# Attention probabilities turned by VectorE block transposes and a DRAM exchange in place of TensorE transposes

## The reference

```
q = (x @ Wq) in 12 heads; k = (x @ Wk), v = (x @ Wv) in 3 heads, repeated 4 times
q, k = apply_rope(q), apply_rope(k)
attn = softmax(q @ k.T * SCALE)      # over the 128 keys (within the 256-key block)
out  = (attn @ v) @ Wo
h = h + attention(layernorm(h))
h = h + gelu(layernorm(h) @ in_weight.T + in_bias) @ out_weight
```

## Time and profile before

| what | value |
|---|---|
| median of 3 runs | 1157.02 us (1156.36 to 1157.75) |
| the profiled execution's own time | 1157.89 us |
| its span, first to last instruction | 1156.1 us |
| mean granted TensorE clock in it | 0.987 of full |
| busy: PE, PE weight load | 1096.8 us, 952.5 us |
| busy: DVE, ACT, POOL | 733.8 us, 758.2 us, 484.8 us |
| DMA | 26.79 MB moved, 23 GB/s over the span |

### The profile page before, as it was taken

The page is one execution under the profiler, slowest core; times in us unless marked ns, Lnnn a source line. Parts: engine busy times, 40 slices in busy tenths (PEclk is TensorE's granted clock), DMA queues, the critical chain, the costliest instruction groups (busy, mean ns, idle before and its releaser), DMA issues.

```text
span 1156.1 us, 24938 instructions
## 1 busy us (share of the span) xinstructions
PE 1096.8 (95%) x8000; PEld 952.5 (82%) x8000; DVE 733.8 (63%) x1999; ACT 758.2 (66%) x2532; POOL 484.8 (42%) x711
## 2 busy tenths in 40 slices
PE   3789999999999999999999999999999999999996
PEld 2578888888888888888888888888888888888875
DVE  3566666666676676676676666666666667667652
ACT  2456676766676766677766677676667676667763
POOL 0343534443444453443454353444344445344341
PEclk8889999999999999999999999999999999999999
DMA  5000101110010110010110010101000011001000
GB/s 158 19 19 9 26 18 25 25 25 7 25 25 18 25 25 16 16 25 18 25 25 25 7 25 18 25 25 25 7 25 22 22 25 25 9 23 25 0 8 14
DMA packets 47775, 26.79 MB, mean 23 GB/s; under 512 B 20752, under 2 KB 47248, under 8 KB 47760
## 3 DMA queue, kind: packets, MB, share of 16 engines
q1 hardware_dynamic: 45472, 23.46, 8.3%
q10 hardware_dynamic: 2288, 3.15, 0.8%
HBM read 20.30 MB, written 6.29 MB: 23 GB/s over the span
## 4 chain that ended last, share of the span: by engine, by line
PE 74%; DVE 8%; ACT 7%; issue 7%; POOL 3%; SPq 0%; DMA 0%; POOLq 0%; DVEq 0%
PE ring L780 11%; PE bank L698 11%; PE bank L640 11%; PE ring L653 8%; PE ring L677 8%; PE ring L609 7%; PE ring L630 5%; PE ring L663 3%; PE bank L721 2%; ACT t_e L300 2%; PE bank L751 2%; ACT t_q L281 2%; POOL rs L349 2%; DVE hn L442 2%; ACT HH L305 1%
## 5 line engine op out<-in xcount | busy, mean ns | idle before, releaser
L262 ACT ACTIVATE E<-ring,m_neg 128x128 f32<-128x128 f32 x768 | 270.5, 393 | 162.3 <-DVE m_neg L475 162.3
L374 POOL TENSOR_TENSOR E<-E,e_rcp 128x512 f32<-128x512 f32 x192 | 194.5, 1038 | 130.8 <-DVE e_rcp L488 130.7
L475 DVE TENSOR_REDUCE m_neg<-ring 128x4 f32<-128x512 f32 x192 | 120.5, 683 | 106.9 <-PE ring L653 106.9
L262 ACT ACTIVATION_READ_ACCUMULATOR E<-ring,m_neg 128x1 f32 x768 | 178.9, 233 | 0.0
L780 PE MATMUL ring<-wo_sb,OT 128*128 128x192 f32 x768 | 138.6, 330 | 0.3 <-ACT OT L274 0.3
L640 PE MATMUL bank<-wout_sb,G 128*128 128x192 f32 x768 | 138.3, 330 | 0.0
L358 POOL TENSOR_TENSOR q_tok<-rot_c,rot_s 128x384 f32<-128x384 f32 x128 | 125.5, 1000 | 7.8 <-DVE rot_s L464 7.8
L780 PEld LDWEIGHTS ring<-wo_sb,OT 128*128 128x128 f32 x768 | 124.7, 190 | 4.5 <-ACT OT L274 0.7
L640 PEld LDWEIGHTS bank<-wout_sb,G 128*128 128x128 f32 x768 | 123.2, 190 | 3.8
L347 POOL TENSOR_SCALAR ve<-mv 128x1 f32<-128x1 f32 x64 | 13.9, 217 | 242.2 <-DVE mv L438 242.2
L394 POOL TENSOR_SCALAR ve<-mv 128x2 f32<-128x2 f32 x32 | 7.3, 227 | 252.0 <-DVE mv L571 252.0
(11 more groups left out here) (110 smaller groups left out, 2567.2 us busy)
## 6 DMA issues: line engine op xcount, KB each, us to landing
x_sb<-in_x_dram SPq DMA_DIRECT2D x64, 192.0 KB, 2.5
out_dram<-out_sb SPq DMA_DIRECT2D x64, 96.0 KB, 2.3
x_sb<-in_x_dram SPq DMA_DIRECT2D x64, 64.0 KB, 2.4
w_raw<-in_w_att_dram ACTq DMA_DIRECT2D x2, 576.0 KB, 5.0
win_raw<-in_w_in_dram ACTq DMA_DIRECT2D x2, 384.0 KB, 6.1
wo_sb<-in_wo_dram ACTq DMA_DIRECT2D x1, 576.0 KB, 7.0
wout_sb<-in_w_out_dram ACTq DMA_DIRECT2D x1, 576.0 KB, 8.3
bqk_row<-in_bq_row_dram SPq DMA_DIRECT2D x1, 64.0 KB, 2.2
```

Source lines behind the costliest of these rows:

```text
L262: last = nc.scalar.activation(E[:, a, s * P:(s + 1) * P], RING[a][:, s * P:(s + 1) * P], ACT.Exp, bias=m_neg[:, a, s:s + 1], accum_out=e_s ...
L374: nc.gpsimd.tensor_tensor(e, e, r, ALU.mult).then_inc(prob_out, 1)
L475: nc.vector.tensor_reduce(m_neg[:, a, REP * g:REP * (g + 1)], RING[a][:, 512 * g:512 * (g + 1)].rearrange("p (h k) -> p h k", k=P), AX_X, ...
```

## The change

The turn of the probabilities leaves PE. Each group of 4 heads is transposed in 32x32 blocks by one DVE instruction from `E` to a new tile `EB`, ordered so that the column block comes first. SP writes `EB` to a DRAM scratch (`spill`), in two pieces for each sequence: heads 0 to 7 (128 partitions of 4 KB, 512 KB) and heads 8 to 11 (256 KB). SP reads each piece back to `ET` in four DMAs, one for each group of 32 partitions (128 KB or 64 KB each), which puts the blocks in their transposed places. Both the spills are issued before the first of the eight reads, and each read waits for its spill's semaphore. The 12 PE transposes of each sequence and the six copies of a step go. `probs_v` waits for the reads (`filled`), and reads `ET` through a view; `heads_out` undoes the order of columns.

The order of every engine is rewritten around it. On PE the steps that stood beside the turn move: `ffn_second(1)` goes to the following step behind `qkv(0)`, `scores(1)` comes before `tok_h` and `ffn_second(0)`, and `probs_v(0)` comes after them. There is one step more at the end (`NP + 1`), which holds only the last feed-forward result. On DVE the three maxima of the second sequence come before `h_next`. Banks `B6` and `B7` swap roles in part. ACT takes the four token-mixer bias steps before the first exponentials, and the scores of the mixer wait for them.

```diff
+        spill = nc.dram_tensor("spill", (2, P, NH * P), F32, kind="Internal").ap()
+            def blocks_moved(a, q):
+                for k, (s0, heads) in enumerate(PIECES):
+                    c = slice(s0 * P, (s0 + heads) * P)
+                    sp.wait_ge(blocks_out, 6 * q + 3 * a + 2 + k)
+                    need(sp, filled[k], 64 * (2 * (q - 1) + a + 1))
+                    sp.dma_start(spill[a, :, c], EB[:, a, c]).then_inc(spilled[k], 16)
+                for k, (s0, heads) in enumerate(PIECES):
+                    c = slice(s0 * P, (s0 + heads) * P)
+                    need(sp, pv_mm, 4 * (q - 1) + 2 * a + k + 1)
+                    sp.wait_ge(spilled[k], 16 * (2 * q + a + 1))
+                    for j in range(NB):
+                        sp.dma_start(ET[j * B32:(j + 1) * B32, a, c].rearrange("r (i e) -> r i e", i=NB),
+                                     spill[a, :, c].rearrange("(i r) (j e) -> j r i e", i=NB, j=NB)[j]
+                                     ).then_inc(filled[k], 16)
...
+                def blocks_turned(a, g, q):
+                    s0, heads = PIECES[g // 2]
+                    h0 = REP * g - s0
+                    dve.wait_ge(prob_out, 6 * q + 3 * a + g + 1)
+                    need(dve, spilled[g // 2], 16 * (2 * (q - 1) + a + 1))
+                    nc.vector.transpose(
+                        EB[:, a, s0 * P:(s0 + heads) * P].rearrange("p (j h c) -> p h j c", j=NB, h=heads)[:, h0:h0 + REP],
+                        E[:, a, 512 * g:512 * (g + 1)].rearrange("p (h j r) -> p h j r", h=REP, j=NB)
+                    ).then_inc(blocks_out, 1)
...
-                def probs_turned(a, g, q):
-                    pe.wait_ge(prob_out, 6 * q + 3 * a + g + 1)
-                    for s in range(REP * g, REP * (g + 1)):
-                        last = nc.tensor.transpose(RING[a][:, s * P:(s + 1) * P], E[:, a, s * P:(s + 1) * P], ident[:])
-                    last.then_inc(ET_mm, 1)
...
                 if ffn:
                     hn_turned()
-                if att:
-                    for g in range(NKV):
-                        probs_turned(0, g, p)
-                if ffn:
-                    ffn_first()
+                    ffn_first((0, 1))
...
                 if att:
-                    for g in range(NKV):
-                        probs_turned(0, g, p)
+                    key_max(1)
                 if tok:
                     dve.wait_ge(h_mm, n + 1)
```

More of the change, by code:

```diff
@@ L220, in store, with step @@
                                  out_sb[(1 - k) * D2:(2 - k) * D2]).then_inc(stored, 16)
+            def step(p, att, ffn, fin, more):
+                if ffn:
+                    blocks_moved(1, p - 1)
+                if fin:
+                    store(p - 2)
+                if more:
+                    load_ahead(p + 2)
+                if att:
+                    blocks_moved(0, p)
             load(0)
@@ L225, in _ @@
                 sp.dma_start(dst[:], src).then_inc(s_const, 16)
[L226 to L229, removed]
+            step(-1, False, False, False, True)
+            step(0, True, False, False, True)
+            step(1, True, True, False, True)
             with sp.Fori(2, NP - 2) as p:
[L231 to L234, removed]
+                step(p, True, True, True, True)
+            step(NP - 2, True, True, True, False)
+            step(NP - 1, True, True, True, False)
+            step(NP, False, True, True, False)
+            step(NP + 1, False, False, True, False)
             sp.wait_ge(stored, 32 * NP)
@@ L297, in step @@
                     tok_vq(0, B6)
+                    tok_vq(1, B7)
+                if att:
+                    score_exp(0, 0)
+                if ffn:
+                    heads_out(1, p - 1)
+                if att:
+                    score_exp(0, 1)
+                    score_exp(0, 2)
+                if tok:
                     act.wait_ge(s_max, n + 1)
@@ L322, in step @@
                     score_exp(1, 0)
+                    score_exp(1, 1)
+                    heads_out(0, p)
                 if tok:
@@ L572, in step @@
                 if att:
-                    dve.wait_ge(h_kept, p + 1)
-                    need(dve, h2_copied, p)
-                    residual(0, 2 * p + 1)
+                    sums_inverted(1, 0, p)
                 if tok:
@@ L610, in group, with step @@
                 return last
-            def step(p, att, tok, ffn):
+            def step(p, att, tok, ffn, fin):
                 n = p + 1
@@ L793, in step @@
                     qkv(0)
+                if fin:
+                    ffn_second(1, p - 2)
                 if tok:
@@ L796, in step @@
                     tok_qk()
-                if ffn:
-                    for g in range(NKV):
-                        probs_turned(1, g, p - 1)
                 if att:
                     qk_turned(0)
-                if ffn:
-                    probs_v(1, p - 1)
+                if tok:
+                    tok_vq()
                 if att:
@@ L813, in step @@
                     hn_turned()
+                    ffn_first((0, 1))
                 if att:
-                    for g in range(NKV):
-                        probs_turned(0, g, p)
+                    qk_turned(1)
                 if ffn:
-                    ffn_first()
+                    ffn_first((2,))
+                if tok:
+                    tok_probs_turned()
+                if att:
+                    scores(1)
+                if tok:
+                    tok_h()
+                if ffn:
+                    ffn_second(0, p - 1)
                 if att:
@@ L821, in step @@
                 if tok:
-                    tok_probs_turned()
-                if att:
-                    qk_turned(1)
-                if tok:
-                    tok_h()
+                    x_turned()
                 if att:
                     output(0, p)
-                    scores(1)
-                if ffn:
-                    ffn_second(0)
-                if tok:
-                    x_turned()
-                if ffn:
-                    ffn_second(1)
             run(pe, step)
```

233 lines of the change are left out of this document (121 added, 112 removed).

## The result

The changed kernel takes 1268.78 us (median of 4 runs, 1265.31 to 1275.07) against 1156.69 of the kernel before: ratio 1.0977, 95% interval 1.0927 to 1.1027. The forecast of 1176 had the right sign and missed the size by 93 us. The profiled execution took 1275.07 us, its span is 1273.2.

The account below looks back on a forecast made before the run. PE was taken as the bound: its step of 34.36 us falls to 30.54, new waits of 4.16 make it 34.70, +10.5 us over 31 distances; with ends of 5.8 and 2.3, 1176 us, own range 1157 to 1192, full range 1135 to 1214.

Parts of the forecast that it names:

- Bound, and what goes: PE, busy 95%, bounds the step; turns of 2.16 and 1.31 and a 0.35 wait go, 34.36 to 30.54 us.
- `HH` and `OT`: New PE waits per step: 0.84 us for `HH` before `ffn_first`, 0.60 us for `OT` of the second sequence.
- `hn`, 0.62: PE waits 0.62 us a step for DVE's `hn`: 3.39 from the end of `output(1)`, only `qkv(1)`, 2.77, over it.
- `xn`, 1.39: PE waits 1.39 us a step for DVE's `xn`, then 0.35 for its second pair; together 1.74, the largest wait.
- The feed-forward result, 0.36: PE's `tok_qk` reuses the bank of `ffn_second(1)` and waits 0.36 us a step for DVE to empty it.
- Transfers and block turns: DVE block turns take 0.69 us each; the DRAM transfers cost nothing in the loop.
- the line for the DMAs: Transfer time taken as 0.004 us a KB: 512 KB 3.95 us, 256 KB 2.95, 128 KB 2.4.
- the last piece: Second sequence's last exchange piece is ready at 10.1 us, wanted by PE at 11.1: 1.0 to spare, near 1.8 by the rule.
- Late blocks: Rival: transfers 2 us slower or SP's issues dearer, `probs_v` waits about 1.0 us a step: 1207 us, chance 0.16.
- The ends: Program's end +5.8 us for the uncovered DRAM path, start +2.3 us for mixer scores waiting on ACT.
- Waits don't add: Rival: other engines get ahead while PE waits at `xn`; `OT`, `hn` and result waits (1.58) vanish: 1128 us, chance 0.20.

Follow-up runs that it names:

- the three places: Changed kernel with POOL waiting for `hn` and split maxima, plus DVE's `out_sb`, `HL` and `XL` moved ahead of a rotation or block turns: 1171.6 us.
- the first experiment: Changed kernel with two waits added on POOL, so its `probs` start only after DVE has finished `hn` and `xn`: 1235.39 us.
- both: Changed kernel with two of the second sequence's maxima moved behind `h_next` on DVE, and POOL's wait for `hn`: 1207.2 us.
- split maxima: Changed kernel with only one maximum of the second sequence before `h_next` on DVE, and the reciprocal releasing `probs(1, 0)` after `xn`: 1256.86 us.
- last block turn later: Kernel of 1171.6 us with the block turn of (1, 2) later on DVE, behind `out_sb` and the last rotation: 1195.06 us.

## Why the prediction was wrong, step by step

- *Bound, and what goes.* PE's 3.82 us went as counted. But "a microsecond taken from PE counts" did not hold in the order of before: without the turn the step at the full clock is the same 34.36, and waits for ACT's `HH` and POOL's `q_tok` take the turns' place.
- *`HH` and `OT`* came out as worked out: from `hn_turned` to `ffn_first` 619.40 - 618.07 = 1.33, and PE's block from the mixer's scores to `output(1)` 1.42 where 0.81 + 0.60 was forecast.
- *`hn`, 0.62.* From the start of `qkv(1)`, 613.50, to 618.07 is 4.57; less its 2.77 the wait is 1.80. **This is the step that failed**, with `xn` below: the sum took both normalises at the length they had beside another order of POOL. The 3.14 us from the residual to the end of `hn` were read from a step of before in which POOL had only two short copies beside it (0.50 and 0.54), and were carried into an order in which POOL starts `probs` in the same instant. The sign was in the rows: the 64-wide `hn` took 0.49 there, where the same operation for `xn` took 0.31. Of the two operations the first takes 1.09 for 0.38, the second 0.98 for 0.31. Nothing in the prediction looked at POOL's row beside DVE's.
- *`xn`, 1.39.* The same step again: 0.71 longer; 632.45 - 629.09 = 3.36, less 1.44 for `probs_v`, is 1.92. The four transposes behind it take 0.78, as forecast (0.44 before and 0.35 more; the prediction's 0.60 - 0.22 is 0.38).
- *The feed-forward result, 0.36.* The block of `tok_qk_rest` and `tok_qk` is 2.45, forecast 1.67: DVE comes to `out_sb` late because residual, rotations and a block turn stand ahead of it. With the order mended the block is 1.97, so 0.3 over the forecast is left and 0.48 was DVE's order.
- *Not foreseen:* the mixer's `tok_vq` waits for `kT` on DVE (1.64 from start to start, 1.29 before).
- Sum of what was missed in a step: 1.18 + 0.53 + 0.78 + 0.35 = 2.84; the two `output` blocks were 1.92 and 1.82 where 2.05 was counted, 0.36 less, and small additions in the other blocks make about 0.4. That is the 37.60 - 34.70 = 2.90. Over 31 distances 90 us, and the three steps of 40.69 9 more: 99, near the 98.6 by which the profiled run (1275.07) stands over the forecast for it (1176.5). The two waits for normalises are 1.71 of the 2.90.
- *Transfers and block turns.* 0.69 for the turn was right; the line for the DMAs was too high for the spills (512 KB 2.7 in place of 3.95). The estimate of 3.2 us that the prediction took from the Trainium skill ("DMA: Bandwidth & Descriptors", Anatomy of one DMA) rests on a fit for DMAs that GpSimd issues, while SP issues these; 2.7 is below it too. For the last piece, 256 KB out and 64 KB back, the same rule gives as an estimate 1.6 us of spare time, not 1.8. Late blocks did not come, and taking the exchange away changed the step by nothing.
- *The ends.* Forecast +5.8 and +2.3. From the last scores to the last `hn_turned` the kernel before takes 16.2 us (1125.57 to 1141.74), the changed one 25.3: +9.1, of which 8.2 is the exchange with the lower clock behind its wait, as the run without it shows. At the start nothing is lost: the third `tok_qk_rest` starts at 70.51 after 70.69. Together 9 for 8, right by luck, with an error each way.
- *The rivals.* "Waits don't add" pointed the wrong way: while PE stands, the waits of the other queues did not shrink. What no rival held was a duration that depends on what runs beside it. With that mechanism taken out and the three places mended, the step is 34.70 us, which is the forecast's figure, but by luck: `xn` and `probs_v(0)` take 1.13 less than forecast, since the maxima are split, and `hn` and the `output` blocks about 0.5 less, while `q_tok` and `k_tok` of the second sequence (0.64), `kT` (0.36), `out_sb` (0.3) and small additions make it up. What the first experiment bears out are the terms for `hn` and `xn` with short normalises.

The experiments put the 97 us between 1268.8 and 1171.6 in two parts: the normalises and the maxima 61.6 (changed kernel to both), the three places 35.6. In steps at the full clock the first part is 37.60 - 35.61 = 1.99 us, 62 us over 31, so the clock hardly enters it. How it divides between the short normalises, the forecast wait that the split took away, and the waits for `HL` and `XL` that came is not separated.

The Trainium skill states the mechanism ("SBUF — State Buffer", SBUF: two separate sides): DVE in a 2-port mode and GpSimd share a pair of ports by an exclusive lock, whoever starts first holds it for the whole instruction, and the other fully blocks. The traces agree: 0.38 became 1.09 beside an operation of 1.04 that began 0.07 earlier. No trace here names the mode of an instruction, so that a normalise runs in such a mode is not shown. By the same section a DVE instruction with at most one SBUF input outside those modes does not contend. The traces agree: in the run of the three places a block turn that began under POOL's two `q_tok` took its ordinary 0.70. (One with two SBUF inputs can contend, it says; the loops here have none.) DVE's row and POOL's:

```profile
587.28 0.70 DVE L527 STREAM_TRANSPOSE EB<-E 128x512 f32<-128x512 f32 x1
```

```profile
586.51 1.96 POOL L396 TENSOR_TENSOR q_tok<-rot_c,rot_s 128x384 f32<-128x384 f32 x2
```

## What to carry to other kernels

A duration read from one order holds in another only while the same engines work beside it: when an order changes, lay DVE's SBUF-to-SBUF scalings next to POOL's rows in the new one, first where PE waits for them. Before an engine is relieved, leave its work out once and time that: here the bare removal cost 1.0% in the old order, so there was nothing in it to gain, and in the order of the three places the kernel without a turn is 1.1% under the kernel before, about the most that a turn elsewhere could gain there. And work on the busiest engine may be the cover of round trips of other engines; count it off only with the cover's price beside it.

## What the runs showed of the hardware

- DVE's 32-bit scaling from SBUF to SBUF (192 wide 0.38 us, 64 wide 0.31) stretches to 1.09 and 0.98 when it begins just behind the start of a POOL operation of 1.0 us (128x512 or 128x384): it ends 0.05 to 0.12 us after that one. POOL's own time does not change (1.04), nor do DVE's block turns (0.70) or its products read from PSUM (0.55) under POOL's. Beside POOL's root on one column (0.58) a 64-wide normalise of the kernel before kept 0.31.
- A block turn of 128x512 in 32-bit, with the heads strided, takes 693 ns, like a copy out of PSUM of that size (677).
- 512 KB to DRAM landed in 2.7 us and 256 KB in 2.6; reads of 128 KB in 2.8 and of 64 KB in 2.3, four of each in a row: here the time to landing hardly grew with the size.
- TensorE's granted clock fell to the lower level (1.2 of 2.4 GHz) in kernels whose PE had a wait of 0.9 to 2.0 us in every step: in every step (split maxima), in two of three (no turn in the order before), in 9 of 30 (both), 6 (POOL after the normalise), 5 (changed kernel) and 3 (no exchange), the program's end left out. A step so hit was 0.8 to 3.1 us longer. The longest wait alone doesn't decide it: with 1.84 in every step the changed kernel kept the full clock in 25 of 30, and with waits of 0.7 to 1.3 us (last block turn later) the first 29 steps kept it. Where no wait in the loop was over 0.7 us (the kernel before, the three places with and without turn) all its steps were alike.
